# Pooling with a user's rows in eight partitions, 32-column weights in four column groups, and normalisation after the pooling

## The chip, the cores and the metric

The kernel runs on one core of a Trainium2 chip. Its time is the device time in microseconds (us). Weights, inputs and outputs lie in the chip's memory (HBM) before and after.

## The reference

Everything is float32. For 1024 users there are 50 history rows of 300 numbers each (`x`) and 200 label rows of 300 numbers (`label_embedding`).

```python
E, K, N = 300, 200, 50

def attn_pool(x, mask, w_a, b_a, w_b):            # x: [b, 50, 300]
    score = exp((x @ w_a + b_a) @ w_b)            # one number a row
    score = where(mask == 0, PAD, score)          # PAD = -2**32 + 1
    p = softmax(score, axis=1)
    return einsum('bne,bn->be', x, p)

mask = sign(sum(abs(x), axis=2))
q1 = attn_pool(x, mask, w1, b1, w2)
q2 = attn_pool(x, mask, w3, b3, w4)
h  = concat([q1, q2], 1) @ w5 + b5                # [b, 300]
f6 = h @ w6 + b6
g  = (v @ v.T)[iu, ju]                            # upper triangle, 44850 pairs
f7 = (h[:, iu] * h[:, ju] * g) @ w7 + b7
out8 = concat([f6, f7], 1) @ w8 + b8
return einsum('bu,bku->bk', out8, label_embedding)
```

## The kernel before

The users are taken in four groups of 256 (`G = 4`, `GB = 2` tiles of 128 users each). A group passes through stages, and a program written out by hand puts stages of neighbouring groups beside each other. There are six stretches, called phases here: -1 (the head), 0, 1, 2, 3, and 4 (the tail). In phases 0 to 3 a loop over 89 **units** (`NU`) runs the pair products of group `ph`: a unit is up to four tiles of 128 pairs. For a unit the vector engine (DVE) multiplies transposed rows of `h` by rows that a DMA brings back from a copy in HBM (`products`, L739: `sring` and `hT` into `cring`, four slots), the scalar engine (ACT) multiplies the unit's rows of `w7` by `g` (`w7_scale`, L600), and TensorE (PE) takes 4 tiles x 2 matmuls with 128x128 weights and 300 columns from them (`unit`, L466). Between the units stand the pooling of group `ph + 1` (none in phase 3), and on DVE the label products of group `ph - 1` (`label_row`, L766; phases 1 to 4, the tail holds nothing else). The head pools group 0, the first thing that must be done.

**Pooling** goes in **halves** of 64 users (four to a group, `GS = 4`, 16 in all). A user's 50 rows lie in two partitions, 25 rows in each (`T = N // 2`), in five chunks of 5 rows (`XT`, `XCH`), in a ring of eight chunk slots (`XSLOTS`). DVE makes two dot products of each row (`score_row`, L679, 50 steps a half, `XROWS`), ACT the sum of absolute values of each (`absolute`, L540, 25 a half). Then ACT takes the exponential (`exps`), DVE masks and takes the maximum, over two partitions by one shuffle with the neighbour (`maxima`, L703), ACT the softmax's exponential with its sum (`softexp`), DVE adds the two partitions' sums, divides, and spreads the weights into matrices [128 partitions x 128 columns], one for each of the 25 rows (`normalise`, L719, `wts`). `pool_chunk` (L435) on PE multiplies: 25 matmuls a half with 128x128 weights and 300 columns, five after each of five units. ACT copies the result (`pools_out`), PE transposes it (`turn`), ACT copies again (`pools_turned`), and after the fourth half `mix` (L444) multiplies by `w5` (18 matmuls); the result is stored to HBM (`rows_out`, on GpSimd's queue) and read back in shifted rows (`s_load`, L302).

What stands where is set by pairs of numbers, (steps after a half's last row in the head, the same in the phases), and every engine walks through the same steps:

```python
        EXP, SOFT, MAX, NORM = (0, -1), (1, 0), (1, 1), (2, 3)
        POOL = [(3, 3 + c) for c in range(XCH)]
        POOL_OUT, TURN, TURN_OUT = (4, 8), (5, 8), (6, 9)
        MIX, MIX_OUT = (7, 10), (8, 11)
        X_LOAD = [(4, 6 + c) for c in range(XCH)]
```

In a phase the x rows are spread over the first 68 units (a half ends with unit 16, 33, 50 and 67), the label rows over units 8 to 88, so that DVE has as many rows in each. In the head a step has `HEAD_ROWS = 5` rows. Loads of x and labels and of `sring` are all issued by SyncE (SP), in one queue, in this order, each after the wait that frees its slot; the loads of `w7` by ACT.

Of the kernel before, what the change touches and what calls it, by code (L numbers as in the profile page):

```python
# [87 lines left out]
def rec_kernel(nc, x, label, w13, w24, w5, w6, w8, bcols, b8, w7p, vleft, vright, out):  # L88
# [10 lines left out]
    T = N // 2  # L99
# [3 lines left out]
    XT = 5  # L103
    XCH = T // XT
    XROWS = 2 * T
    XSLOTS = 8
# [11 lines left out]
    HEAD_ROWS = 5  # L118
# [4 lines left out]
    with ctx:  # L123
# [17 lines left out]
        wts = sb("wts", [P, T, 2, P // 2])  # L141
# [6 lines left out]
        onehot = sb("onehot", [P, P // 2])  # L148
# [5 lines left out]
        small = sb("small", [P, 3, 2, 3 * T + 8])  # L154
        junk = sb("junk", [P, 2, 2, E], BF16)
        absjunk = sb("absjunk", [P, 2, E], BF16)
        absum = sb("absum", [P, 3, T])
        masked = sb("masked", [P, 3, T])
# [35 lines left out]
        prob_done = sem("prob_done")  # L194
# [15 lines left out]
        dots = [small[:, k, :, 0:T] for k in range(3)]  # L210
        expo = [small[:, k, :, T:2 * T] for k in range(3)]
        prob = [small[:, k, :, 2 * T:3 * T] for k in range(3)]
        maxi = [small[:, k, :, 3 * T:3 * T + 1] for k in range(3)]
        maxo = [small[:, k, :, 3 * T + 1:3 * T + 2] for k in range(3)]
        nmax = [small[:, k, :, 3 * T + 2:3 * T + 3] for k in range(3)]
        part = [small[:, k, :, 3 * T + 3:3 * T + 4] for k in range(3)]
        parto = [small[:, k, :, 3 * T + 4:3 * T + 5] for k in range(3)]
        total = [small[:, k, :, 3 * T + 5:3 * T + 6] for k in range(3)]
        recip = [small[:, k, :, 3 * T + 6:3 * T + 7] for k in range(3)]

        x_v = x.rearrange("(s b) (f t) e -> s (b f) t e", b=P // 2, f=2)
# [6 lines left out]
        HEAD_STEPS = GS * XROWS // HEAD_ROWS  # L228
        TAIL_STEPS = GB * LC

# [40 lines left out]
        def last_step(ph):  # L271
            return {-1: x_end(-1, GS - 1) + 14, G: TAIL_STEPS}.get(ph, NU)
# [12 lines left out]
        def _(sp):  # L285
# [5 lines left out]
            def x_load(n):  # L291
                s, c = n // XCH, n % XCH
                sp.dma_start(xring[:, n % XSLOTS], x_v[s, :, c * XT:(c + 1) * XT, :]).then_inc(x_in[n % XSLOTS], 16)
# [42 lines left out]
            for n in range(XSLOTS):  # L336
                x_load(n)
# [8 lines left out]
            for ph in range(-1, G + 1):  # L346
# [5 lines left out]
                for u in range(last_step(ph)):  # L352
# [12 lines left out]
                    for c in range(XCH):  # L365
                        for s in after_half(ph, u, *X_LOAD[c]):
                            n = ((ph + 1) * GS + s) * XCH + c
                            if n + XSLOTS < NS * XCH:
                                sp.wait_ge(x_used, n + 1)
                                x_load(n + XSLOTS)  # L370

        @block.gpsimd
        def _(pool):
# [8 lines left out]
            step(nc.gpsimd.memset(onehot[:], 0.0))  # L382
            step(nc.gpsimd.affine_select(out=ident[:], in_=ident[:], compare_op=ALU.not_equal, fill=1.0,
                                         base=0, pattern=[[-1, P]], channel_multiplier=1))
            for f in range(2):
                step(nc.gpsimd.affine_select(out=onehot[:], in_=onehot[:], compare_op=ALU.not_equal,
                                             fill=1.0, base=-f, pattern=[[-2, P // 2]], channel_multiplier=1))
# [31 lines left out]
        def _(pe):  # L419
# [242 lines left out]
        def _(dve):  # L662
# [37 lines left out]
            def carry():  # L700
                nc.vector.memset(tick[:], 0.0)
# [139 lines left out]
```

## Time and profile before

| | |
|---|---|
| median of three runs | 2047.17 us (2040.95 to 2052.43) |
| the profiled execution | 2043.87 us |
| its span on the core | 2041.7 us |
| PE busy (matmuls) | 1760.3 us, 86% |
| DVE busy | 1455.3 us, 71% |
| ACT busy | 863.3 us, 42% |
| DMA | 629.75 MB, 308 GB/s over the span |
| pooling matmuls, records on PE | 800 |
| x score rows on DVE | 800 |

A float32 matmul leaves two records on PE, each with a weight load (LDWEIGHTS, engine PEld) of its own: 400 pooling matmuls are 800 records. The engines work beside each other, so their busy times don't add up to the span; what counts is which of them the others wait for in a given phase. The head lasts from 0 to 164.3 us, the phases 0 to 3 end at about 588, 1033, 1482 and 1868 us, and the tail is the rest.

### The profile page before, as it was taken

The numbers are of one execution on the slowest core, as the hardware profiler recorded it, in microseconds if no ns is written. First come the engines' busy times: TensorE is split into PE (matmuls) and PEld (weight loads), VectorE is DVE, ScalarE is ACT, GpSimd is POOL, SyncE is SP. The second block draws the span as 40 slices with busy tenths as digits, with TensorE's granted clock in tenths as the row PEclk, the third lists the DMA queues.
The fourth block names the chain that finished last, engine by engine and source line by source line (L and its number), as shares of the span: only waits on it lengthen the run. The fifth ranks groups of instructions, "written<-read, shape, count | busy, mean of one in ns | idle before, by whom it ended". The sixth has DMA issues, their size and how long they took to land.

```text
span 2041.7 us, 23493 instructions
## 1 busy us (share of the span) xinstructions
PE 1760.3 (86%) x6820; PEld 1290.3 (63%) x6820; DVE 1455.3 (71%) x5499; ACT 863.3 (42%) x2413; POOL 22.7 (1%) x49
## 2 busy tenths in 40 slices
PE   3567999999999999999979999999889999998000
PEld 2345777777767777777657777777667777775000
DVE  8835645544147888988558898888536777773998
ACT  3525545545345564553345454553234444442000
POOL 0000000000000000000000000000000000000000
PEclk9788999999999999999989999999899999997555
DMA  6358566666566999999968999989869999995997
GB/s 223 126 165 315 190 234 238 219 242 237 193 240 241 359 354 379 354 382 405 350 246 303 361 340 392 348 340 389 273 252 356 404 406 408 409 391 178 392 395 310
DMA packets 121789, 629.75 MB, mean 308 GB/s; under 512 B 14136, under 2 KB 24921, under 8 KB 99133
## 3 DMA queue, kind: packets, MB, share of 16 engines
q1 hardware_dynamic: 93853, 408.04, 53.0%
q10 hardware_dynamic: 26208, 217.10, 28.0%
q0 software_dynamic: 1600, 3.10, 0.5%
q8 instruction: 55, 0.90, 0.2%
q14 instruction: 73, 0.60, 0.1%
HBM read 625.09 MB, written 3.10 MB: 308 GB/s over the span
## 4 chain that ended last, share of the span: by engine, by line
PE 79%; DVE 11%; DMA 6%; ACT 2%; issue 2%; POOL 0%; SPq 0%; DVEq 0%; ACTq 0%; POOLq 0%
PE bank L480 64%; PE bank L440 10%; DVE lring L775 8%; DMA sring<-hrows 3%; DMA lring<-in_label 2%; DMA wring<-in_w7p 2%; PE bank L452 1%; DVE junk L688 1%; ACT absjunk L546 1%; PE bank L462 1%; PE bank L490 1%; PE bank L488 1%; DVE cring L755 1%; ACT wring L608 1%; PE bank L432 0%
## 5 line engine op out<-in xcount | busy, mean ns | idle before, releaser
L480 PE MATMUL bank<-wring,cring 128*128 128x300 f32 x5616 | 1448.2, 419 | 38.9 <-DVE cring L755 38.2
L480 PEld LDWEIGHTS bank<-wring,cring 128*128 128x128 f32 x5616 | 1072.7, 192 | 398.7 <-DVE cring L755 40.1
L608 ACT ACTIVATE wring<-wring,gcol 128x300 f32<-128x300 f32 x1404 | 642.0, 532 | 786.6 <-PE bank L480 497.2
L755 DVE TENSOR_TENSOR cring<-hT,sring 128x1024 f32<-128x1024 f32 (+1 forms) x344 | 418.1, 1216 | 432.6 <-PE bank L480 386.6
L775 DVE SCALAR_TENSOR_TENSOR lring<-lring,out 128x300 f32<-128x300 f32 x1600 | 644.7, 465 | 29.9 <-DMA lring<-in_label 16.2
L688 DVE SCALAR_TENSOR_TENSOR junk<-xring,ubc 128x300 bf16<-128x300 f32 x800 | 328.1, 463 | 0.0
L440 PE MATMUL bank<-xring,wts 128*128 128x300 f32 x800 | 221.4, 429 | 64.9 <-DVE wts L733 64.9
L440 PEld LDWEIGHTS bank<-xring,wts 128*128 128x128 f32 x800 | 157.0, 197 | 119.2 <-issue 59.7
L546 ACT ACTIVATE absjunk<-xring 128x300 bf16<-128x300 f32 x400 | 174.9, 439 | 0.2
L775 DVE DVE_READ_ACCUMULATOR lring<-lring,out 128x1 f32 x1600 | 129.9, 81 | 0.0
L546 ACT ACTIVATION_READ_ACCUMULATOR absjunk<-xring 128x1 f32 x400 | 75.4, 189 | 0.0
L688 DVE DVE_READ_ACCUMULATOR junk<-xring,ubc 128x1 f32 x800 | 64.3, 80 | 0.0
L733 DVE TENSOR_TENSOR wts<-small,onehot 128x640 f32<-128x640 f32 x80 | 60.2, 819 | 0.6
L755 DVE TENSOR_TENSOR cring<-sring 128x1024 f32<-128x1024 f32 (+1 forms) x12 | 11.5, 956 | 62.4 <-issue 43.9
L535 ACT ACTIVATE flat<-bank 128x300 f32<-128x300 f32 x24 | 9.6, 414 | 108.8 <-PE bank L440 91.5
L452 PE MATMUL bank<-poolT,w5sb 128*128 128x256 f32 (+1 forms) x144 | 39.3, 403 | 0.7 <-issue 0.7
L707 DVE TENSOR_SCALAR masked<-absum 128x25 f32<-128x25 f32 x16 | 2.9, 178 | 42.6 <-ACT absjunk L546 33.4
L452 PEld LDWEIGHTS bank<-poolT,w5sb 128*128 128x128 f32 (+1 forms) x144 | 20.2, 164 | 19.1 <-issue 16.3
L432 PE MATMUL bank<-ident,flat 128*128 128x128 f32 (+1 forms) x72 | 12.9, 304 | 15.3 <-ACT flat L535 15.3
L432 PEld LDWEIGHTS bank<-ident,flat 128*128 128x128 f32 (+1 forms) x72 | 8.5, 140 | 21.4 <-ACT flat L535 19.1
L462 PE MATMUL bank<-hT,w6sb 128*128 128x256 f32 (+3 forms) x72 | 19.5, 399 | 0.0
L560 ACT ACTIVATE small<-small 128x25 f32<-128x25 f32 x32 | 9.8, 308 | 22.6 <-DVE small L717 22.6
(49 smaller groups left out, 182.9 us busy)
## 6 DMA issues: line engine op xcount, KB each, us to landing
lring<-in_label SPq DMA_DIRECT2D x320, 750.0 KB, 7.2
wring<-in_w7p ACTq DMA_DIRECT2D x168, 1200.0 KB, 8.0
sring<-hrows SPq DMA_DIRECT2D x172, 512.0 KB
xring<-in_x SPq DMA_DIRECT2D x80, 750.0 KB, 5.8
wring<-in_w7p ACTq DMA_DIRECT2D x8, 1050.0 KB, 8.1
sring<-hrows SPq DMA_DIRECT2D x16, 176.0 KB
sring<-hrows SPq DMA_DIRECT2D x16, 132.0 KB
sring<-hrows SPq DMA_DIRECT2D x8, 160.0 KB
```

The costliest lines, as they stand in the source:

```text
L432: mm = pe.transpose(dst[0:n, c * P:(c + 1) * P], src[:, o:o + n], ident[:])
L440: mm = pe.matmul(pooled[s % 2][:, 0:E], wts[:, t].rearrange("p h b -> p (h b)"), xring[:, (s * XCH + c) % XSLOTS, t % XT, :], start=(t == ...
L452: mm = pe.matmul(dst[0:n, 0:L], w5sb[0:nk, q, o:o + n], poolT[0:nk, q % NCH, q // NCH, :], start=(q == 0), stop=(q == 2 * NCH - 1))
L462: mm = pe.matmul(dst[0:n, 0:L], w6sb[0:nk, c, o:o + n], hT[0:nk, g % 2, c, :], start=(c == 0), stop=(c == NCH - 1))
L480: mm = pe.matmul(acc[(g * GB + b) % 4][:, 0:E], lhs, w, start=(t == 0), stop=(t == NT - 1))
L488: pe.matmul(dst[:, 0:E], f6T[0:n, c, b * P:(b + 1) * P], w8sb[0:n, c, :], start=False, stop=False)
L546: nc.scalar.activation(absjunk[:, k % 2, :], xring[:, n % XSLOTS, t % XT, :], ACT.Abs, accum_out=absum[:, s % 3, t:t + 1]).then_inc(abs_do ...
L608: ins = nc.scalar.activation(w, w, ACT.Copy, scale=gcol[:, t:t + 1])
L688: ins = nc.vector.scalar_tensor_tensor(out=junk[:, k % 2, r % 2, :], in0=xring[:, n % XSLOTS, t % XT, :], scalar=1.0, in1=ubc[:, hd, 0:E], ...
L733: nc.vector.tensor_tensor(wts[:, t0:t1], prob[k][:, :, t0:t1].rearrange("p h t -> p t h").unsqueeze(3).to_broadcast([P, XT, 2, P // 2]), o ...
L755: nc.vector.tensor_tensor(cut(cring[:, k % CSLOTS]), in0, cut(sring[:, nb % SSLOTS]), ALU.mult).then_inc(c_ready, 1)
L775: ins = nc.vector.scalar_tensor_tensor(out=row_in, in0=row_in, scalar=1.0, in1=out8[:, m % (2 * GB), :], op0=ALU.mult, op1=ALU.mult, accum ...
```

## The change

A user's 50 rows now lie in **eight** partitions (`FOLD = 8`), six in each, and the two rows left over in a seventh place of the first two of the eight; the seventh place of the other six is set to zero once, at the start. A half of 64 users becomes four **parts** of 16 users (`PARTS`, `UB`), each a chunk of seven rows (`XT = 7`) in a ring of six (`XSLOTS`). A half has 28 places a partition and not 25 (`TT`), and so 56 score rows and 28 sums of absolute values. The weights of one place are a matrix [128 x 32]; the matmul of part j writes partitions 32j to 32j + 31 of the PSUM bank, and the four parts of a place follow each other on PE.

A chunk comes with three DMAs: one of six rows for all partitions, and two of one row for 16 partitions each. At the start the six large ones are issued first and the twelve small ones behind them. The maximum now goes over eight partitions (three shuffles), and is subtracted on DVE. The weights are not normalised: DVE writes them in one instruction and sums them (`weights`), PE adds four small matmuls (2 columns) that sum over partitions, and after the pooling DVE takes the denominator and its reciprocal (`denominators`), which ACT applies when it copies the pooled rows.

```diff
-    XT = 5
-    XCH = T // XT
-    XROWS = 2 * T
-    XSLOTS = 8
+    FOLD = 8
+    UB = P // FOLD
+    M = 2 * UB
+    PARTS = P // 2 // UB
+    TM, LEFT = N // FOLD, N % FOLD
+    T = TM + 1
+    TT = PARTS * T
+    CUTS = [(0, T)] if T <= 7 else [(0, 7), (7, T)]
+    CHUNK = [(j, t0, t1) for j in range(PARTS) for t0, t1 in CUTS]
+    XT = max(t1 - t0 for _, t0, t1 in CHUNK)
+    XCH = len(CHUNK)
+    XROWS = 2 * TT
+    XSLOTS = 6
-    HEAD_ROWS = 5
+    HEAD_ROWS = 7
...
-        EXP, SOFT, MAX, NORM = (0, -1), (1, 0), (1, 1), (2, 3)
-        POOL = [(3, 3 + c) for c in range(XCH)]
-        POOL_OUT, TURN, TURN_OUT = (4, 8), (5, 8), (6, 9)
-        MIX, MIX_OUT = (7, 10), (8, 11)
-        X_LOAD = [(4, 6 + c) for c in range(XCH)]
+        EXP, SOFT, MAX, WEIGH = (0, 0), (1, 1), (1, 1), (2, 2)
+        POOL, DEN, POOL_OUT = (2, 3), (3, 4), (3, 4)
+        TURN, TURN_OUT = (4, 5), (4, 6)
+        MIX, MIX_OUT = (5, 7), (5, 8)
+        X_LOAD = (3, 4)
...
-                sp.dma_start(xring[:, n % XSLOTS], x_v[s, :, c * XT:(c + 1) * XT, :]).then_inc(x_in[n % XSLOTS], 16)
+                if main:
+                    rows = src[:, 0:FOLD * TM, :].rearrange("b (f t) e -> b f (t e)", f=FOLD)
+                    z = min(t1, TM)
+                    sp.dma_start(slot[:, 0:z - t0, :].rearrange("p t e -> p (t e)"),
+                                 rows[:, :, t0 * E:z * E]).then_inc(s, 16)
+                if left and t1 == T:
+                    for f in range(LEFT):
+                        sp.dma_start(slot[f:P:FOLD, TM - t0, :], src[:, FOLD * TM + f, :]).then_inc(s, 16)
...
             for n in range(XSLOTS):
-                x_load(n)
+                x_load(n, left=False)
+            sp.wait_ge(vconsts, 1)
+            for n in range(XSLOTS):
+                x_load(n, main=False)
...
-                    for c in range(XCH):
-                        for s in after_half(ph, u, *X_LOAD[c]):
+                    for s in after_half(ph, u, *X_LOAD):
+                        sp.wait_ge(x_used, (ph + 1) * GS + s + 1)
+                        for c in range(XCH):
                             n = ((ph + 1) * GS + s) * XCH + c
                             if n + XSLOTS < NS * XCH:
-                                sp.wait_ge(x_used, n + 1)
                                 x_load(n + XSLOTS)
...
-            def pool_chunk(s, c):
-                if c == 0 and s >= 2:
+            def pool_rows(s):
+                if s >= 2:
                     pe.wait_ge(pool_out, s - 1)
-                pe.wait_ge(wts_done, s * XCH + c + 1)
-                for t in range(c * XT, (c + 1) * XT):
-                    mm = pe.matmul(pooled[s % 2][:, 0:E], wts[:, t].rearrange("p h b -> p (h b)"),
-                                   xring[:, (s * XCH + c) % XSLOTS, t % XT, :], start=(t == 0), stop=(t == T - 1))
+                pe.wait_ge(wts_done, 2 * (s + 1))
+                dst = pooled[s % 2]
+                for t in range(T):
+                    for j in range(PARTS):
+                        c = next(c for c in range(XCH) if CHUNK[c][0] == j and CHUNK[c][1] <= t < CHUNK[c][2])
+                        pe.matmul(dst[j * M:(j + 1) * M, 0:E], wts[:, j * T + t].rearrange("p h b -> p (h b)"),
+                                  xring[:, (s * XCH + c) % XSLOTS, t - CHUNK[c][1], :], start=(t == 0), stop=(t == T - 1))
+                for j in range(PARTS):
+                    mm = pe.matmul(dst[j * M:(j + 1) * M, E:E + 2], both[:].rearrange("p h b -> p (h b)"),
+                                   part[s % 3][:, :, j], start=True, stop=True)
                 mm.then_inc(x_used, 1)
...
             def pools_out(s):
-                act.wait_ge(x_used, (s + 1) * XCH)
-                cp(flat[:, s % 2, :], pooled[s % 2][:, 0:E]).then_inc(pool_out, 1)
+                act.wait_ge(den_done, 2 * (s + 1))
+                nc.scalar.activation(flat[:, s % 2, :], pooled[s % 2][:, 0:E], ACT.Copy,
+                                     scale=den[:, s % 2, 1:2]).then_inc(pool_out, 1)
...
+            def denominators(n):
+                dve.wait_ge(x_used, n + 1)
+                nc.vector.scalar_tensor_tensor(
+                    out=denjunk[:], in0=pooled[n % 2][:, E:E + 2], scalar=1.0, in1=headmask[:], op0=ALU.mult,
+                    op1=ALU.mult, accum_out=den[:, n % 2, 0:1]).then_inc(den_done, 1)
+                dve.wait_ge(den_done, 2 * n + 1)
+                nc.vector.reciprocal(den[:, n % 2, 1:2], den[:, n % 2, 0:1]).then_inc(den_done, 1)
```

**PE, phase 0.** L440 and L469 are the pooling, L480 and L512 the units, L432 and L457 the transposes, L472 the small sums. Before, from the last chunk of the first half to the first of the second:

```order
L440 MATMUL bank<-xring,wts 128x300 x5
L480 MATMUL bank<-wring,cring 128x300 x8
L432 MATMUL bank<-ident,flat 128x128 x2
L432 MATMUL bank<-ident,flat 44x128
L480 MATMUL bank<-wring,cring 128x300 x96
L440 MATMUL bank<-xring,wts 128x300 x5
L480 MATMUL bank<-wring,cring 128x300 x8
```

Now, from before the first half's pooling to the second's:

```order
L512 MATMUL bank<-wring,cring 128x300 x72
L469 MATMUL bank<-xring,wts 32x300 x28
L472 MATMUL bank<-small,both 32x2 x4
L512 MATMUL bank<-wring,cring 128x300 x16
L457 MATMUL bank<-ident,flat 128x128 x2
L457 MATMUL bank<-ident,flat 44x128
L512 MATMUL bank<-wring,cring 128x300 x120
```

Five groups of five matmuls with a unit between them became one group of 28 and one of four.

**DVE, head, end of the first half.** L717 and L758 end the maximum, L688 and L728 are score rows, L733 and L767 write the weights. Before:

```order
L717 TENSOR_SCALAR small<-small 128x2
L688 SCALAR_TENSOR_TENSOR junk,small<-xring,ubc 128x300 x5
L701 MEMSET tick 128x1
L723 STREAM_SHUFFLE small<-small 128x2
L724 TENSOR_TENSOR small<-small 128x2
L725 RECIPROCAL small<-small 128x2
L726 TENSOR_TENSOR small<-small 128x2x25
L733 TENSOR_TENSOR wts<-small,onehot 128x640 x5
L688 SCALAR_TENSOR_TENSOR junk,small<-xring,ubc 128x300 x45
```

Now:

```order
L758 TENSOR_TENSOR small<-small 128x2x28
L728 SCALAR_TENSOR_TENSOR junk,small<-xring,ubc 128x300 x7
L767 TENSOR_TENSOR wts<-small,onehot 128x896
L770 TENSOR_REDUCE small<-small 128x2x4
L728 SCALAR_TENSOR_TENSOR junk,small<-xring,ubc 128x300 x7
L775 SCALAR_TENSOR_TENSOR denjunk,den<-bank,headmask 128x2
L779 RECIPROCAL den<-den 128x1
L728 SCALAR_TENSOR_TENSOR junk,small<-xring,ubc 128x300 x42
```

The normalisation in front of the weights is gone, and L775, seven rows behind the weights, waits for the pooling on PE.

**SP, phase 0, the x loads behind the first half.** L311 and L337 load `sring`. Before:

```order
L311 DMA sring<-hrows 128x1024 [waits c_ready] x11
L293 DMA xring<-in_x 128x1500 [waits x_used]
L311 DMA sring<-hrows 128x1024 [waits c_ready]
L293 DMA xring<-in_x 128x1500 [waits x_used] x2
L311 DMA sring<-hrows 128x1024 [waits c_ready]
L293 DMA xring<-in_x 128x1500 [waits x_used] x2
```

Now:

```order
L337 DMA sring<-hrows 128x1024 [waits c_ready] x10
L315 DMA xring<-in_x 128x1x1800 [waits x_used]
L319 DMA xring<-in_x 16x300 x2
L315 DMA xring<-in_x 128x1x1800
L319 DMA xring<-in_x 16x300 x2
```

Five loads, each behind its own chunk's matmuls, became a block of four chunks (twelve DMAs) behind one wait.

## Rows read from the trace of the kernel before

**Rows 1.** Costliest groups: line engine op, xcount | busy us, mean ns | idle before.
```profile
L480 PE MATMUL bank<-wring,cring 128*128 128x300 f32 x5616 | 1448.2, 419 | 38.9 <-DVE cring L755 38.2
L775 DVE SCALAR_TENSOR_TENSOR lring<-lring,out 128x300 f32<-128x300 f32 x1600 | 644.7, 465 | 29.9 <-DMA lring<-in_label 16.2
L440 PE MATMUL bank<-xring,wts 128*128 128x300 f32 x800 | 221.4, 429 | 64.9 <-DVE wts L733 64.9
```

**Rows 2.** Windows: length; busy PE, PEld, DVE, ACT, POOL; clock, DMA, GB/s.
```profile
0.00:164.30 164.30, 74.44 (x252) 50.19 (x252) 106.41 (x493) 62.91 (x263) 5.69 (x17) 0.83 0.53 183
164.30:588.00 423.70, 423.66 (x1669) 314.90 (x1670) 210.27 (x585) 204.86 (x573) 4.21 (x8) 0.99 0.64 230
588.00:1033.00 445.00, 433.61 (x1705) 319.22 (x1704) 356.99 (x1362) 216.24 (x606) 4.76 (x9) 0.99 0.91 345
1033.00:1482.00 449.00, 435.49 (x1703) 320.47 (x1702) 361.50 (x1376) 215.19 (x603) 5.30 (x11) 0.98 0.89 335
```

**Rows 3.** Timeline of PE, phase 1, a unit and chunks: start us, us.
```profile
944.73 4.20 PE L480 MATMUL bank<-wring,cring 128*128 128x300 f32 x16
948.77 2.69 PE L440 MATMUL bank<-xring,wts 128*128 128x300 f32 x10
951.30 4.20 PE L480 MATMUL bank<-wring,cring 128*128 128x300 f32 x16
```

**Rows 4.** Timeline of PEld in phase 0: the mix, loads of changing shape.
```profile
541.80 0.73 PEld L452 LDWEIGHTS bank<-poolT,w5sb 128*128 128x128 f32 x4 [0.33 <-issue]
542.87 0.29 PEld L452 LDWEIGHTS bank<-poolT,w5sb 44*128 44x128 f32 x2 [0.33 <-issue]
543.49 0.59 PEld L452 LDWEIGHTS bank<-poolT,w5sb 128*44 128x44 f32 x4 [0.33 <-issue]
```

**Rows 5.** Weight loads by shape, whole run: busy us, mean ns.
```profile
L440 PEld LDWEIGHTS bank<-xring,wts 128*128 128x128 f32 x800 | 157.0, 197 | 119.2 <-issue 59.7 <-DVE wts L733 12.1
L452 PEld LDWEIGHTS bank<-poolT,w5sb 128*44 128x44 f32 x32 | 3.2, 119 | 4.5 <-issue 2.9
```

**Rows 6.** Timeline of PE, head: poolings, mix, first unit.
```profile
38.00 15.46 PE L440 MATMUL bank<-xring,wts 128*128 128x300 f32 x50 [30.28 <-DVE wts L733]
66.37 14.96 PE L440 MATMUL bank<-xring,wts 128*128 128x300 f32 x50 [11.85 <-DVE wts L733]
120.86 15.00 PE L440 MATMUL bank<-xring,wts 128*128 128x300 f32 x50 [10.85 <-DVE wts L733]
137.59 9.88 PE L452 MATMUL bank<-poolT,w5sb 128*128 128x256 f32 x36 [0.67 <-issue]
164.34 5.86 PE L480 MATMUL bank<-wring,cring 128*128 128x300 f32 x12 [16.87 <-DVE cring L755]
```

**Rows 7.** Timeline of DVE, head, first half: rows, maximum, weights.
```profile
11.32 0.46 DVE L688 SCALAR_TENSOR_TENSOR junk<-xring,ubc 128x300 bf16<-128x300 f32 x1
11.71 0.46 DVE L688 SCALAR_TENSOR_TENSOR junk<-xring,ubc 128x300 bf16<-128x300 f32 x1
32.86 0.17 DVE L707 TENSOR_SCALAR masked<-absum 128x25 f32<-128x25 f32 x1
33.95 0.16 DVE L716 TENSOR_TENSOR small<-small 128x2 f32<-128x2 f32 x1
34.22 0.46 DVE L688 SCALAR_TENSOR_TENSOR junk<-xring,ubc 128x300 bf16<-128x300 f32 x1
37.03 3.77 DVE L733 TENSOR_TENSOR wts<-small,onehot 128x640 f32<-128x640 f32 x5
```

**Rows 8.** DMA, 0 to 30 us: KB, median us to landing; x ring.
```profile
DMA packets 3254, 9.42 MB, mean 314 GB/s; under 512 B 464, under 2 KB 1965, under 8 KB 3253
xring<-in_x SPq DMA_DIRECT2D x8, 750.0 KB, 11.7
wring<-in_vleft ACTq DMA_DIRECT2D x1, 702.0 KB, 4.2
DMA to landing us min/median/max: 4.1/5.8/16.4
```

**Rows 9.** Waits on DVE, 940 to 1070 us: us, times, longest.
```profile
DVE lring L775 <- DMA lring<-in_label: 11.5, 6, 3.1
```

**Rows 10.** Timeline of DVE, then PE, end of phase 1.
```profile
1005.19 1.23 DVE L755 TENSOR_TENSOR cring<-sring 128x1024 f32<-128x1024 f32 x1 [3.57 <-issue]
1024.95 1.23 DVE L755 TENSOR_TENSOR cring<-sring 128x1024 f32<-128x1024 f32 x1 [14.25 <-issue]
1026.23 7.22 PE L480 MATMUL bank<-wring,cring 128*128 128x300 f32 x20 [9.55 <-DVE cring L755]
```

More of the change, by code:

```diff
@@ L98, in rec_kernel @@
     L = GB * P
-    T = N // 2
     NS = 2 * NBT
     GS = 2 * GB
-    XT = 5
-    XCH = T // XT
-    XROWS = 2 * T
-    XSLOTS = 8
+    FOLD = 8
[11 more added lines that the diff above has]
+    XSLOTS = 6
+    ROUNDS = [1 << k for k in range(FOLD.bit_length() - 1)]
     LR = 5
@@ L208, in rec_kernel, with x_landed @@
         out_stored = [sem(f"out_stored{k}") for k in range(2)]
[L210 to L221, printed above, removed]
+        dots = [small[:, k, :, 0:TT] for k in range(3)]
+        expo = [small[:, k, :, TT:2 * TT] for k in range(3)]
+        prob = [small[:, k, :, 2 * TT:3 * TT] for k in range(3)]
+        maxi = [small[:, k, :, 3 * TT:3 * TT + PARTS] for k in range(3)]
+        maxo = [small[:, k, :, 3 * TT + PARTS:3 * TT + 2 * PARTS] for k in range(3)]
+        part = [small[:, k, :, 3 * TT + 2 * PARTS:3 * TT + 3 * PARTS] for k in range(3)]
+        by_part = lambda a: a.rearrange("p h (j t) -> p h j t", t=T)
+        x_v = x.rearrange("(s b) n e -> s b n e", b=UB)
         label_v = label.rearrange("(m p) (c r) e -> m p c r e", p=P, r=LR)
         out_v = out.rearrange("(m p) k -> m p k", p=P)
-        HEAD_STEPS = GS * XROWS // HEAD_ROWS
         TAIL_STEPS = GB * LC
+        ROWS = [(c, t, hd) for c, (_, t0, t1) in enumerate(CHUNK) for t in range(t0, t1) for hd in range(2)]
+        def x_landed(n):
+            loads = lambda m: 1 + LEFT if CHUNK[m % XCH][2] == T else 1
+            return 16 * sum(loads(m) for m in range(n % XSLOTS, n + 1, XSLOTS))
         def x_rows_by(ph, u):
@@ L505, in _ @@
                         unit(ph, u)
-                    for c in range(XCH):
-                        for s in after_half(ph, u, *POOL[c]):
-                            pool_chunk((ph + 1) * GS + s, c)
+                    for s in after_half(ph, u, *POOL):
+                        pool_rows((ph + 1) * GS + s)
                     for s in after_half(ph, u, *TURN):
@@ L674, in _ @@
             dve.wait_ge(u_ready, 2)
-            dve.wait_ge(consts, 5)
-            SWAP = [q ^ 1 for q in range(32)]
+            dve.wait_ge(consts, 2)
+            nc.vector.tensor_reduce(onehot[:], ident[:].rearrange("p (u f) -> p u f", f=FOLD), AX.X,
+                                    ALU.add).then_inc(vconsts, 1)
+            nc.vector.tensor_reduce(headmask[:], ident[:].rearrange("p (j h u) -> p h j u", h=2, u=UB), AX.XY,
+                                    ALU.add).then_inc(vconsts, 1)
+            dve.wait_ge(vconsts, 6)
+            nc.vector.tensor_copy(both[:], onehot[:].unsqueeze(1).to_broadcast([P, 2, UB])).then_inc(vconsts, 1)
+            dve.wait_ge(vconsts, 7)
             def score_row(s, r):
-                c, hd, t = r // (2 * XT), r % (2 * XT) // XT, r // (2 * XT) * XT + r % XT
+                c, t, hd = ROWS[r]
+                at = CHUNK[c][0] * T + t
                 n = s * XCH + c
-                if r % (2 * XT) == 0:
-                    dve.wait_ge(x_in[n % XSLOTS], 16 * (n // XSLOTS + 1))
-                k = s * T + r // 2
+                if t == CHUNK[c][1] and hd == 0:
+                    dve.wait_ge(x_in[n % XSLOTS], x_landed(n))
+                k = s * TT + r // 2
                 if r % 2 == 0 and k >= 2:
@@ L720, in normalise, with weights @@
+            def weights(n):
                 k = n % 3
                 dve.wait_ge(prob_raw, n + 1)
[L722 to L727 removed]
@@ L728, in normalise @@
[L728 to L737 removed]
+                if n >= 1:
+                    dve.wait_ge(x_used, n)
@@ L790, in _ @@
                         maxima((ph + 1) * GS + s)
-                    for s in after_half(ph, u, *NORM):
-                        normalise((ph + 1) * GS + s)
+                    for s in after_half(ph, u, *WEIGH):
+                        weights((ph + 1) * GS + s)
+                    for s in after_half(ph, u, *DEN):
+                        denominators((ph + 1) * GS + s)
 def kernel(**inputs):
```

104 lines of the change are left out of this document (49 added, 55 removed).

## The prediction

> **What bounds the kernel now.** I read the windows by phase first. In phases 0 to 2 PE is busy for all but 0, 11 and 14 us, at a granted clock of 0.98 to 0.99 of 2.4 GHz, so there PE sets the pace; DVE stands beside it with 210 us in phase 0 but 357 and 362 us in phases 1 and 2 (80%), where DMA moves 345 and 335 GB/s at a share of 0.9 [rows 2]. In the head PE is busy for 74 of 164 us. There the timeline has the poolings 26.5 to 28.4 us after one another, each waiting for DVE's weights [rows 6], and DVE makes score rows without a gap [rows 7]: the head is DVE's, up to the last pooling. Of PE's time the units' records hold 1448 us and the pooling's 800 records 221 [rows 1]; a gain can only come from the latter. Phase 3 and the tail have no pooling and stay as they are. So the change can gain on PE in the 12 halves of phases 0 to 2, and act on the head through DVE, the x loads and the last pooling.
>
> **PE, the pooling.** Now ten records (five matmuls) take from 948.77 to 951.30 us, 0.2525 us a record, and a unit of 16 records 4.04 us at the same pitch [rows 3]. A half costs 50 x 0.2525 = 12.6 us. The change makes 28 matmuls of it, 56 records. The trace has no two matmuls that lie on different columns of the array, so the price is bounded. From above, one after another: 56 x 0.2525 = 14.1 us, since it is the 300 columns that pass through that cost, not the width of the weights (in the mix two records more of 256 columns cost 1.07 - 0.62 = 0.45 us, whatever the shape [rows 4]). From below, all four parts at once: 14.1 / 4 = 3.5 us. I take the middle way, two at once, 7.1 us: the two records of one matmul need the same 32 columns and stand one behind the other in the queue, so if PE starts matmuls in the order of the queue, only the second record of one part and the first of the next can run together. Then come the four small matmuls, 8 records: below, nearly nothing; above, one narrow weight load of 0.119 us each [rows 5], 0.95 us; I take 0.7. And the array changes shape twice a half: in the mix four records of 128 rows and two of 44 take 1.07 + 0.62 = 1.69 us, where six at 0.225 would take 1.35, so a switch costs 0.17 us [rows 4], two of them 0.35. Together P = 8.2 us a half (bounds 4.6 and 15.4) in place of 12.6. **12 halves: -53 us** (bounds -96, +34).
>
> The Trainium skill (TensorE: Matmul & The Clock Gate, The mechanism) says that a weight load overlaps a running matmul only where the row groups differ, and all groups here have the same 128 rows. The rows speak against it: loads of 0.197 us for the same 128 rows lie under records that follow each other every 0.2525 us [rows 3, 5]. By the rule each record would have its load of about 0.119 us on top, 56 x 0.37 = 21 us a half, and the 12 halves would cost 100 us and not gain; I leave that out of the sum.
>
> **The head.** Five steps.
> (1) The rows start later. Before they start at 11.3 us [rows 7]. Now the small loads of the first chunk stand in the queue behind six large ones: 6 x 128 x 7200 bytes = 5.5 MB, and 1.4 MB of `vleft` and `vright`, 7.0 MB. The 9.42 MB of the first 30 us came in about 22 us [rows 8], some 415 GB/s, so they land at 2 + 17 = 19 us. Rows start at 19.3, +8.
> (2) A row costs 0.392 us on DVE (11.32 to 11.71 [rows 7]); 56 take 22.0 us and not 19.6.
> (3) Between the last row and the pooling stand two steps of 7 rows (2.7 us each, before 2.0), the maximum, 1.36 us now (32.86 to 34.22 [rows 7]) and 0.8 more for two shuffles and maxima (0.2 each with their gaps), and the weights: 896 columns in one instruction, about 1.0 us by 0.75 for 640 (3.77 for five [rows 7]), and a small sum, 1.3. First pooling: 19.3 + 22.0 + 2.7 + 2.2 + 2.7 + 1.3 = 50.2 us, before 38.0 [rows 6].
> (4) The halves follow each other more slowly. Six slots hold one and a half halves; the third and fourth chunk of a half are loaded only after the whole pooling of the half before. So the period is: P in the head; the third chunk with its three DMAs, 4.8 us (shortest landing 4.1 [rows 8], with 0.96 MB for 0.77 and three issues); 28 rows, 11.0; then 2.7 + 2.2 + 2.7 + 1.3 as above: 24.7 + P. In the head PE comes from a long wait and begins at its lower level (1.2 GHz): the poolings take 15.0 us there for 12.6, so I add 2.4 to P, 10.6 (the head's granted clock is 0.83 [rows 2]). Period 35.3 us, before 27.6 (three from 38.0 to 120.86 [rows 6]).
> (5) Behind the last half there are no rows between, -5.5: last pooling from 50.2 + 3 x 35.3 - 5.5 = 150.6 to 161.2 us, before to 135.9. The denominators put 0.5 us in front of the copy. From there to the first unit (28.5 us now [rows 6]) nothing changes.
> **Head: +26 us.** In general 4P - 7.
>
> **Phases 1 and 2, the loss of DVE's lead.** DVE may be four units ahead of PE (`CSLOTS`). Now `denominators` makes it wait in each half for the pooling behind the unit just before; from there it is 4.0 - 0.5 - 1.2 = 2.3 us ahead. In phase 0 it wins the lead back at once. In phases 1 and 2 a step is a product (1.15) and 7.4 rows, 4.05 us, against a unit's 4.04: it does not. What the lead covered comes to PE: maxima and weights of the next half, 3.5 us against 2.3, 1.2 x 6 = 7 us; waits for label loads, 11.5 us at the end of phase 1 [rows 9]; and at a phase's end the products of unit 86 at 1005.2 us, from which the last `sring` loads take 20 us, a wait of 9.6 us on PE already [rows 10], which 5 us less lead makes 5 longer, twice. The block of four x chunks (3.8 MB, some 10 us of DMA at these rates) stands in SP's queue ahead of labels and `sring`, which have 20 us to come; covered, if barely. Bounds 5 and 45; **+20 us**, near the lower one because the pooling itself is still 8 us in which DVE can work.
>
> Nothing: DVE's weights (five instructions less one, 2.7 us a half, against 6 more rows, 2.4 us), ACT's three more sums of absolute values, 2 us a half on an engine with half its time free in every phase [rows 2].
>
> **Sum:** -53 + 26 + 20 = -7 us against the profiled execution's 2043.9, 2037. That execution lies 3.3 us under the median of the runs, so I give **2040 us**. With P open the sum is 16P - 158 + the loss of lead (20): the change gains if a half's pooling takes less than 8.6 us. My forecast sits on that point, and half a per cent, 10 us, is what a measurement of this kernel can tell from no change.
>
> **Rivals.**
> *All four parts run together.* P = 4.6. For it: the parts touch neither each other's columns nor partitions. Against: the two records of a matmul share their columns and stand together in the queue. -96 us on PE, the head 4 x 4.6 - 7 = +11; but DVE with 17 steps of 4.05 and 4 us of maxima and weights, 73 us a half, now stands level with PE (17 x 4.04 + 4.6), so the lost lead costs 35: 1995 us, as a median 1998. The Trainium skill gives 2.38 times for three column tiles (TensorE: Matmul & The Clock Gate, Measured speedup vs the span model), which for four would be nearer to this case than to mine; no row here shows it.
> *The parts run one after another*, the case that ends slower. P = 15.4: +34 on PE, head +55, lost lead 5 to 10 (DVE has more time): 2140 us. For it: no row shows two matmuls at once, and all four write the same PSUM bank. It decides from P over 9.2 us on.
> *The pairs overlap only in part*, P about 11: +16 x 11 - 158 + 15 = 2077, as a median 2080.
> *The side effects are not as I take them:* the small x loads don't wait behind the large ones (-8), the lead is kept (-15): 2014 to 2017, inside my own range.
>
> **Chances.** Two at once 0.50, four at once 0.14, one after another 0.22, in part 0.14. The forecast's own range is 2015 to 2075. The whole range, 1985 to 2125, leaves out most of the serial case, a little of the fastest one, and the tails. Faster by over half a per cent: 0.22 of the forecast's half (where the lead or the first loads cost less) and 0.13, 0.35. Within: 0.20. Slower: 0.10 of the forecast's, 0.21 of the serial, 0.14 in part, 0.45.
>
> **What would show it.** The time from the first pooling record of a half in phase 0 to the next unit's first: 8.2 us, 4.6 or 15.4. In the head: first score row at 19.3 us, first pooling at 50, period 35, last pooling's end at 161, first unit at 190. In phases 1 and 2: PE waits for DVE's products after the poolings, DVE for PE at the denominators, phase 0 shorter by 18 us and phases 1 and 2 by 8 each. Wrong would be the argument on the queue's order if P is under 6 or over 10, and the one on slots if the head's period is under 30 us.

## The result and the profile after

The changed kernel takes **2098.4 us** (median of four runs, 2088.8 to 2103.6) beside 2045.6 us for the kernel before on the same chip: a ratio of **1.024, 95% interval 1.021 to 1.027**. It is slower. I had forecast 2040 us, a hair faster, in a range up to 2125. One of the ten runs of e2 below took 4978 us; its ratio is made without it.

The busy times by phase, in the columns of [rows 2]:

```profile
0.00:195.75 195.75, 37.22 (x309) 18.07 (x309) 109.31 (x545) 68.24 (x281) 5.06 (x14) 0.76 0.61 152
195.75:603.00 407.25, 393.17 (x1726) 286.04 (x1726) 208.95 (x635) 207.87 (x587) 4.21 (x8) 0.98 0.73 239
603.00:1070.00 467.00, 407.65 (x1742) 290.34 (x1740) 347.94 (x1378) 219.03 (x620) 4.76 (x9) 0.95 0.93 326
1070.00:1520.00 450.00, 408.03 (x1760) 291.86 (x1760) 359.28 (x1421) 219.23 (x619) 5.30 (x10) 0.96 0.92 335
```

PE is no longer busy throughout the phases: 14, 59 and 42 us of them are idle, where there were 0, 11 and 14. The head grew from 164.3 to 195.75 us. For exact lengths I take one mark in each phase, the transposes of `flat7` in unit 1: from the first unit to the first mark phase 0 takes 419.0 us (before 433.3), from mark to mark phase 1 takes 477.0 (449.4) and phase 2 takes 451.7 (448.7), phase 3 369.7 (373.4). With the head's 31.4 that is -14, +28, +3, -4 and +31, in all +44 of the 45 us by which the span of the profiled execution grew (between the medians lie 53 us).

The pooling on PE reaches the lower bound that the prediction had for its records, 3.5 us. Timeline of PE in phase 0, to be read against [rows 3], and below it the first 0.05 us of the same half by themselves:

```profile
282.11 3.74 PE L469 MATMUL bank<-xring,wts 128*32 128x300 f32 x56
285.66 0.22 PE L472 MATMUL bank<-small,both 128*32 128x2 f32 x8
285.81 8.35 PE L512 MATMUL bank<-wring,cring 128*128 128x300 f32 x32
```
```profile
281.76 0.42 PE L512 MATMUL bank<-wring,cring 128*128 128x300 f32 x1
282.11 0.46 PE L469 MATMUL bank<-xring,wts 128*32 128x300 f32 x4
```

From 282.11 to 285.81 us are **3.7 us a half**, the small matmuls included, where it was 12.6. All four parts run at once: four records start within 20 ns of each other, the next four 0.25 us later, and so on (56 records in 3.55 us, 0.063 us each on average, a quarter of 0.2525). Over 12 halves PE is given 107 us. They are lost again, and more. Who waits for whom on PE and DVE, whole run (us, times, longest):

```profile
DVE cring L797 <- DMA sring<-hrows: 139.8, 14, 30.8
...
PE bank L512 <- DVE cring L797: 127.6, 30, 20.0
...
DVE lring L817 <- DMA lring<-in_label: 75.0, 19, 26.6
...
DVE junk L728 <- DMA xring<-in_x: 30.5, 4, 17.5
```

PE waited 38 us for products before and now 128; behind the products stand the loads of `sring`, labels and x. The head shows what is wrong with them. The DMA of the first 34 us, in 40 slices (busy share, then GB/s), of the kernel before and then of the changed one:

```profile
DMA  0088999999999999999999999999996000000000
GB/s 0 8 140 350 416 423 416 406 409 445 416 417 409 438 431 409 416 438 409 409 424 409 424 412 363 371 342 298 308 319 178 24 0 0 0 0 0 10 0 0
```
```profile
DMA  0178999998999999998999999999999999799999
GB/s 0 6 107 366 416 397 409 291 202 215 263 229 271 195 271 246 237 246 212 263 229 271 195 263 220 220 246 237 254 212 254 246 271 215 157 221 223 201 250 376
...
xring<-in_x SPq DMA_DIRECT2D x6, 900.0 KB, 18.0
xring<-in_x SPq DMA_DIRECT2D x12, 18.8 KB, 22.5
```

`vleft` and `vright` come at 410 GB/s in both. Then the x loads come at 410 GB/s before and at **about 235 GB/s** now, and the DMA engines are as busy with it (share 0.9). By the trace's packet records each packet takes longer: one of 7200 bytes 0.51 us here (median from 8 to 18 us), and 0.27 us in e1 and e6 below. The first score row is at 31.4 us, where I had said 19.3:

```profile
31.40 0.47 DVE L728 SCALAR_TENSOR_TENSOR junk<-xring,ubc 128x300 bf16<-128x300 f32 x1 [17.46 <-DMA xring<-in_x]
```

So the question of the experiments: does the halved rate of the x loads make the whole loss, and what halves it? The rivals are my own terms, the lead of DVE and the block of x loads in SyncE's queue.

### The profile page after: what moved, and what is told of

The parts are those of the page before. It is cut to its first block, busy times and chain, and to the rows that moved or that the text cites. A ratio compares the mean times of both kernels' runs of the same rounds, so it can differ in the third digit from the quotient of the medians.

```text
span 2087.0 us, 24279 instructions
## 1 busy us (share of the span) xinstructions
PE 1645.0 (79%) x7044; PEld 1175.4 (56%) x7044; DVE 1453.0 (70%) x5695; ACT 878.5 (42%) x2477; POOL 22.0 (1%) x46
## 3 DMA queue, kind: packets, MB, share of 16 engines
q10 hardware_dynamic: 26208, 217.10, 28.2%
## 4 chain that ended last, share of the span: by engine, by line
PE 47%; DVE 26%; DMA 20%; SPq 3%; issue 3%; ACT 1%; POOL 0%; DVEq 0%; ACTq 0%; POOLq 0%
PE bank L512 39%; DVE lring L817 13%; DMA sring<-hrows 8%; DMA lring<-in_label 8%; DVE junk L728 6%; DVE cring L797 5%; PE bank L469 3%; DMA xring<-in_x 2%; SPq L319 2%; DMA wring<-in_w7p 2%; PE bank L484 1%; PE bank L494 1%; SPq L315 1%; PE bank L522 1%; PE bank L520 1%
## 5 line engine op out<-in xcount | busy, mean ns | idle before, releaser
L512 PE MATMUL bank<-wring,cring 128*128 128x300 f32 x5616 | 1466.6, 423 | 130.2 <-DVE cring L797 127.6
L512 PEld LDWEIGHTS bank<-wring,cring 128*128 128x128 f32 x5616 | 1079.7, 193 | 505.8 <-DVE cring L797 141.9
L728 DVE SCALAR_TENSOR_TENSOR junk<-xring,ubc 128x300 bf16<-128x300 f32 x896 | 365.9, 463 | 30.5 <-DMA xring<-in_x 30.5
L580 ACT ACTIVATE absjunk<-xring 128x300 bf16<-128x300 f32 x448 | 195.9, 438 | 17.9 <-DMA xring<-in_x 17.6
L469 PE MATMUL bank<-xring,wts 128*32 128x300 f32 x896 | 67.6, 458 | 127.8 <-DVE small L770 127.8
L469 PEld LDWEIGHTS bank<-xring,wts 128*32 128x32 f32 x896 | 30.4, 120 | 162.7 <-issue 117.1
L580 ACT ACTIVATION_READ_ACCUMULATOR absjunk<-xring 128x1 f32 x448 | 84.1, 188 | 0.0
L728 DVE DVE_READ_ACCUMULATOR junk<-xring,ubc 128x1 f32 x896 | 71.6, 80 | 0.0
L775 DVE SCALAR_TENSOR_TENSOR denjunk<-bank,headmask 128x2 f32<-128x2 f32 x16 | 2.5, 159 | 80.9 <-PE bank L472 80.9
L597 ACT ACTIVATE flat<-bank,den 128x300 f32<-128x300 f32 x16 | 8.2, 512 | 62.4 <-DVE den L779 62.4
L457 PE MATMUL bank<-ident,flat 128*128 128x128 f32 (+1 forms) x72 | 13.2, 308 | 20.3 <-ACT flat L567 16.1
L457 PEld LDWEIGHTS bank<-ident,flat 128*128 128x128 f32 (+1 forms) x72 | 8.6, 141 | 24.8 <-ACT flat L567 17.9
L520 PE MATMUL bank<-w8sb,f6T 128*128 128x300 f32 (+1 forms) x48 | 19.2, 527 | 0.0
```

What stands on the lines that cost most here:

```text
L457: mm = pe.transpose(dst[0:n, c * P:(c + 1) * P], src[:, o:o + n], ident[:])
L469: pe.matmul(dst[j * M:(j + 1) * M, 0:E], wts[:, j * T + t].rearrange("p h b -> p (h b)"), xring[:, (s * XCH + c) % XSLOTS, t - CHUNK[c][1] ...
L512: mm = pe.matmul(acc[(g * GB + b) % 4][:, 0:E], lhs, w, start=(t == 0), stop=(t == NT - 1))
L520: pe.matmul(dst[:, 0:E], f6T[0:n, c, b * P:(b + 1) * P], w8sb[0:n, c, :], start=False, stop=False)
L580: nc.scalar.activation(absjunk[:, k % 2, :], xring[:, n % XSLOTS, t - CHUNK[c][1], :], ACT.Abs, accum_out=absum[:, s % 3, at:at + 1]).then ...
L728: ins = nc.vector.scalar_tensor_tensor(out=junk[:, k % 2, r % 2, :], in0=xring[:, n % XSLOTS, t - CHUNK[c][1], :], scalar=1.0, in1=ubc[:, ...
```

## The experiments

Times are medians beside the kernel before on the same chip (2044.7, 2045.6 and 2046.4 us in the three groups).

**e1, the load as one flat list.** The large load's source, 16 users x 8 pieces, becomes 128 pieces at one pitch. This variant reads other rows of x than the reference asks for, the same number of bytes in the same pieces.

```diff
-                    rows = src[:, 0:FOLD * TM, :].rearrange("b (f t) e -> b f (t e)", f=FOLD)
+                    rows = bass.AP(x.tensor, part0, [[TM * E, P], [1, TM * E]])
```

> The changed kernel, but each large x load reads 128 equal pieces of 7200 bytes one behind another (one pitch for all partitions) in place of 16 users by 8 pieces; it reads other rows than the reference's, and the small loads stay. Theory A (the x loads run at some 230 GB/s and not 415 because of how the load is described, users by pieces, and not for their size): the head's first score row comes at about 22 us and not at 32, the x loads go at about 400 GB/s, the head ends 15 to 20 us earlier, the whole is 20 to 45 us faster than the changed kernel. Theory B (7200-byte pieces, or reading from a close region, are slow in themselves): nothing changes, within 10 us of the changed kernel.

Measured: **1984.3 us**, ratio 0.972 (0.968 to 0.975), 114 us below the changed kernel and 3% below the one before. The head's DMA, same slices:

```profile
GB/s 0 6 189 344 416 420 407 436 420 432 407 415 441 466 407 415 424 415 407 415 424 443 277 178 291 171 337 378 311 284 205 37 10 0 0 0 0 10 0 0
```

Some 420 GB/s as long as the large x loads run (to 18 us), with pieces of 7200 bytes, from a region as close together. So it is neither the size of the pieces nor the closeness of what is read. Theory A stands so far; its gain was 114 us and not 20 to 45.

**e2, the kernel before with a load in two levels.** 64 users x 2 pieces of 6000 bytes; it reads rows 24 to 48 in place of 25 to 49.

```diff
-                sp.dma_start(xring[:, n % XSLOTS], x_v[s, :, c * XT:(c + 1) * XT, :])
+                rows = bass.AP(x.tensor, s * (P // 2) * N * E + c * XT * E, [[N * E, P // 2], [(T - 1) * E, 2], [1, XT * E]])
+                sp.dma_start(xring[:, n % XSLOTS].rearrange("p t e -> p (t e)"), rows)
```

> The kernel before, with its x loads described as 64 users by two pieces (the second piece begins one row early, so that the two levels can't be merged; it is the same number of bytes in pieces of the same 6000 bytes, but rows 24 to 48 in place of 25 to 49). Theory A: the first x loads fall from 415 to about 230 GB/s, and the kernel gets 10 to 40 us slower by that alone. Theory B: the time is that of the kernel before, within 5 us.

Measured: 2045.3 us, ratio 1.000 (0.998 to 1.002), and no lower rate in the head:

```profile
GB/s 0 6 162 311 416 416 424 410 437 409 431 409 431 424 409 431 409 438 409 409 417 416 438 405 360 340 354 290 299 330 192 38 6 0 0 0 0 0 10 0
```

Theory A as I had put it falls: two levels alone cost nothing. What is left of it is the number at the outermost level, 64 here and 16 in the change.

**e5, the kernel before with 16 x 8.** As e2 with 16 groups x 8 pieces of 6000 bytes, the groups a row closer than in the reference, so it too reads other rows.

```diff
+                rows = bass.AP(x.tensor, s * (P // 2) * N * E + c * XT * E, [[4 * N * E - E, 16], [T * E, 8], [1, XT * E]])
```

> The kernel before, with each x load described as 16 groups by 8 pieces of 6000 bytes (the groups begin one row early so that the levels can't be merged; same bytes, other rows). Theory A16 (the slow rate belongs to an outermost level of 16, so that each DMA engine gets eight neighbouring partitions; an outermost level of 64, as in the run before, does not have it): the x loads fall to about 230 GB/s in the head, the first score rows are on time or up to 2 us late, and the kernel is 10 to 60 us slower than before. Theory size (it is the 7200-byte pieces, or 57.6 KB of neighbouring reads for an engine): the time is that of the kernel before, within 5 us, and the head's rate 410 GB/s.

Measured: **2095.4 us**, ratio 1.023 (1.018 to 1.027). The kernel before, with its old pooling, its old normalisation and its old order, loses 50 us by this one description. Its DMA in the head, and PE's waits:

```profile
GB/s 0 6 107 379 416 416 418 284 210 254 219 240 226 233 219 240 226 240 226 254 226 240 226 240 233 240 226 233 219 233 229 226 233 240 254 226 261 193 217 270
```
```profile
PE bank L482 <- DVE cring L757: 70.6, 12, 17.5
```

The same 235 GB/s (230 here), with pieces of 6000 bytes that lie 30 KB apart; theory size falls. The first score row is only 1.2 us late (12.5 us), since the first chunk is alone in front. By the marks the head and phase 0 lose 3 and 2 us, phase 1 loses 45 and phase 2 loses 8. PE waits 71 us for products in place of 38.

**e6, the change with halves of users.** Each user is cut into two halves of 25 rows first, and each half into four partitions of 6 rows and one left over. The load's outermost level is then 32, and the rows left over are one load of 32 partitions. All rows are there: the softmax and the pooling do not care in which partition of its user a row lies.

```diff
-                    rows = src[:, 0:FOLD * TM, :].rearrange("b (f t) e -> b f (t e)", f=FOLD)
+                    rows = bass.AP(x.tensor, part0, [[N // 2 * E, 2 * UB], [TM * E, FOLD // 2], [1, TM * E]])
...
-                    for f in range(LEFT):
-                        sp.dma_start(slot[f:P:FOLD, TM - t0, :], src[:, FOLD * TM + f, :]).then_inc(s, 16)
+                    sp.dma_start(slot[0:P:FOLD // 2, TM - t0, :],
+                                 bass.AP(x.tensor, last, [[N // 2 * E, 2 * UB], [1, E]])).then_inc(s, 16)
```

> The changed kernel with a user's rows split first into two halves of 25 and each half into four partitions of six and one row left over. A large load is then 32 half users by 4 pieces of 7200 bytes, and the two small loads of a chunk become one of 32 partitions. All rows are the reference's. Theory A16: the x loads run at some 400 GB/s as in the flat load, SyncE issues 8 x loads a half and not 12, and the time is 1975 to 1990 us, 3% below the kernel before. Theory size: 2070 to 2100 us, as the changed kernel.

Measured: **1986.9 us**, ratio 0.970 (0.967 to 0.973). The rate in the head is 410 to 440 GB/s while the large x loads run; phase 0 takes 399.1 us by the marks, phase 1 436.3, phase 2 427.1, the head 174.5:

```profile
51.41 5.93 PE L469 MATMUL bank<-xring,wts 128*32 128x300 f32 x56 [43.33 <-DVE small L770]
82.75 5.62 PE L469 MATMUL bank<-xring,wts 128*32 128x300 f32 x56 [23.77 <-DVE small L770]
113.79 5.47 PE L469 MATMUL bank<-xring,wts 128*32 128x300 f32 x56 [23.76 <-DVE small L770]
140.01 6.00 PE L469 MATMUL bank<-xring,wts 128*32 128x300 f32 x56 [19.11 <-DVE small L770]
174.48 30.90 PE L512 MATMUL bank<-wring,cring 128*128 128x300 f32 x113 [16.22 <-DVE cring L797]
```

Against the changed kernel the head is 21 us shorter and the phases 20, 41 and 25. e1, with two small loads a chunk, and e6, with one, end within 3 us of each other, so the second small load has no price that shows here.

**e3, the parts one after another.** The pooling's two loops swapped, so that neighbours in PE's queue use the same 32 columns.

> The changed kernel with the two loops of the pooling swapped: all seven places of a part one after another, so that neighbours in the queue use the same 32 columns. If overlap needs different columns in neighbours, a half's 56 records take 14.1 us in the phases in place of 3.6, or somewhat less at the seams. If the four-fold rate were owed to the narrow weights alone, 3.6 us stay. The whole then is about 12 x 10 = 120 us slower at most.

Measured: 2204.0 us, ratio 1.078 (1.073 to 1.084). Timeline of PE, the same half:

```profile
315.75 10.63 PE L469 MATMUL bank<-xring,wts 128*32 128x300 f32 x53
325.97 0.24 PE L472 MATMUL bank<-small,both 128*32 128x2 f32 x6
326.22 0.92 PE L469 MATMUL bank<-xring,wts 128*32 128x300 f32 x3
327.10 8.35 PE L512 MATMUL bank<-wring,cring 128*128 128x300 f32 x32
```

11.35 us a half in place of 3.7, so the four-fold rate is owed to neighbours on different columns, not to narrow weights. And six records of the small matmuls, which stand behind in the queue, run at 325.97 us while three of the pooling still follow at 326.22: matmuls on different columns pass each other. That is also why it is 11.35 and not 14.1: in the trace's records, at each of the three seams, the first four records of the next part start beside the last four of the part before, which saves 12 x 0.2525 = 3.0 us.

**e4, the denominators later.** In the changed kernel, in the phases:

```diff
-        POOL, DEN, POOL_OUT = (2, 3), (3, 4), (3, 4)
-        TURN, TURN_OUT = (4, 5), (4, 6)
-        MIX, MIX_OUT = (5, 7), (5, 8)
+        POOL, DEN, POOL_OUT = (2, 3), (3, 7), (3, 7)
+        TURN, TURN_OUT = (4, 8), (4, 9)
+        MIX, MIX_OUT = (5, 10), (5, 11)
```

> The changed kernel with the denominators, the copy, the transposes and the mix three steps later in the phases (the head as it is). Theory lead (DVE's wait for the pooling takes its lead, and PE then waits for products): PE's wait for DVE falls from 128 us by 40 or more, the whole is 20 to 40 us faster. Theory queue (the block of twelve x loads holds up the loads of sring and labels behind it in SyncE's queue): PE's wait stays within 20 us of 128, and the whole within 12 us of the changed kernel.

Measured: 2099.0 us, ratio 1.026 (1.023 to 1.030), the changed kernel's time; PE waits 134 us for products. The lead was not it. That is what theory queue had said too, but this run doesn't test the block itself: it leaves the twelve loads where they are.

**e7 and e8, on top of e6.** e7 issues each small load behind its own large one at the start. e8 also takes e4's edit and spreads the four chunks' loads over four steps:

```diff
-        X_LOAD = (3, 4)
+        X_LOAD = [(3, 7 + c) for c in range(XCH)]
```

> As the halves kernel, and at the start each chunk's small load stands right behind its large one, not behind all six. Expected: the first score row at 11 to 13 us in place of 21, the first pooling at about 43, and the whole 8 us faster than the halves kernel. Rival: DVE then waits for later chunks instead, and under 3 us are gained.

> As the kernel with halves and small loads first, with the denominators, copy, transposes and mix three steps later in the phases, and the four chunks' x loads issued in four steps (7 to 10 after the half) in place of one block. With the loads at full rate the lost lead and the block are what is left: if they cost what the prediction said, 10 to 20 us faster than without; if the rate of the x loads was all of it, within 5 us, or slower since the last chunks now come later than DVE needs them.

Measured: e7 **1978.2 us**, ratio 0.966 (0.963 to 0.969), its first score row at 12.3 us and its first pooling at 43.3 us against 51.4: 8.1 us in the trace, 8.8 in the medians, as expected. e8: 1978.3 us, 0.967 (0.963 to 0.970). DVE's waits at the denominators fall from 81.5 us in e7 to 20.8, yet PE's wait for products stays (65.6 and 64.5): the lead has no price here either. The block was moved in the same run, and DVE waited 25.6 us for x in place of 6.3; so a small gain from spreading it may be hidden, and alone it was not tried.

**e9 to e11, the slots.** e9 is e7 with seven chunk slots (`w1T` lies in `wring` for its short life, which frees the room). e10 is e9, and e11 is e7, with `HEAD_ROWS = 4`.

> As the kernel with halves and small loads first, with seven chunk slots in place of six (w1 lies for its short life in the ring of w7). The prediction's step on the slots: the head's period, 31.1 us now, is set by the third chunk of a half, which is loaded only after the pooling of the half before. With seven slots only the fourth chunk waits, and DVE has 14 rows more (5.5 us) to hide it: period about 28 us, the head 8 us shorter, the whole 1970 us. Rival: DVE's own work (56 rows, 22 us, and its wait at the denominators, 7 us) holds the period at 29.5 or more, and 4 us or less are gained.

> As the seven slots, with 4 rows a step in the head and not 7. The rows that stand between a half's last row and its weights, and between the weights and the denominators, fall from 7 to 4 each: the pooling starts 2.4 us earlier in each half, and if the wait for the fourth chunk binds, the period shortens by as much, 7 us over the head; DVE waits longer at the denominators, so if DVE's own work binds, nothing is gained or 3 us are lost.

> Six slots, 4 rows a step in the head. Here the load behind the pooling binds by the prediction's step 4, so the period falls by 2 x 3 rows, 2.4 us, three times, 5 to 7 us in all: 1971 us. If DVE's own work binds, 1978 us stay.

Measured: e9 **1959.4 us, ratio 0.958 (0.956 to 0.961)**, e10 1964.1 (0.960, 0.956 to 0.963), e11 1978.1 (0.968, 0.964 to 0.971). The poolings of e9's head:

```profile
43.36 5.13 PE L467 MATMUL bank<-xring,wts 128*32 128x300 f32 x56 [35.34 <-DVE small L768]
71.58 6.36 PE L467 MATMUL bank<-xring,wts 128*32 128x300 f32 x56 [21.45 <-DVE small L768]
101.14 5.25 PE L467 MATMUL bank<-xring,wts 128*32 128x300 f32 x56 [21.54 <-DVE small L768]
125.18 5.18 PE L467 MATMUL bank<-xring,wts 128*32 128x300 f32 x56 [17.15 <-DVE small L768]
158.77 45.41 PE L510 MATMUL bank<-wring,cring 128*128 128x300 f32 x172 [16.17 <-DVE cring L795]
```

The periods fall from e7's 31.5, 31.0 and 26.4 us to 28.2, 29.6 and 24.0, and the first unit comes at 158.8 us, where e7 has 167.3 and e6 174.5: the 8 us that were expected. Behind the head, by the marks, phase 1 takes 433.9 us (e7 437.9), phase 2 424.0 (425.3) and phase 3 368.7 (373.2). Phase 3 pools nothing and no run changes it, but over the thirteen traces it takes 365.3 to 374.4 us, so differences of this size can't be laid to the slot.

In the heads the traces show which wait the edits touch. DVE waits for x 6.3 us in e7, and not at all in e9, e10 and e11; at the denominators it waits 16.1, 14.7, 20.0 and 19.3 us (e7, e9, e10, e11). The first units come at 167.3, 158.8, 164.4 and 164.2 us: e11's shorter steps take the wait for x away and lengthen the other one by 3.2, which leaves 3 us in the head and nothing in the medians (1978.1 against 1978.2), and in e10 there is no wait for x left to win, only the longer one. e10 is 5 us slower than e9 in the medians, inside both intervals.

e9 is the fastest version: 87 us (4.2%) below the kernel before, 139 below the change.

## Why the prediction was wrong

*The pooling on PE (forecast 8.2 us a half, 53 us gained).* Measured 3.7, 107 us given to PE. The step that failed is the premise that PE starts matmuls in the order of its queue, so that only two could overlap. Four records start together at 282.11 us, and e3 shows it again: records on other columns overtake. The rival with all four at once had 4.6 us and the right mechanism; I gave it 0.14. Its time, 1998 us, is near that of e6, 1987, where the x loads have their rate back. Here the Trainium skill's figure for column tiles (TensorE: Matmul & The Clock Gate, Measured speedup vs the span model) pointed the right way, and the measured factor for four is 4.0. The Trainium skill's rule that a weight load overlaps a running matmul only where the row groups differ (TensorE: Matmul & The Clock Gate, The mechanism), which I had left out of the sum, does not hold here: the 56 loads of a half, 0.11 us each (6.2 us in all), lie within the 3.55 us of its 56 records.

*What carries the result, the rate of the x loads, is not in the prediction.* With PE's 107 us and the head's 31 as measured, the sum needs 123 us lost in phases 0 to 2, where I had 20. The prediction took 415 GB/s for the x loads, from rows of the kernel before, whose load is described otherwise: 128 pieces at one pitch. The diff shows the new description, and I counted its bytes and not its shape. With a 16 at the outermost level the rate is 235 GB/s, so the 14.7 MB of large loads in the head and in each of three phases take 63 us of all 16 DMA engines and not 36. Where DMA had spare time (phase 0, share 0.64) it costs waits for `sring` behind the block, 20 us by e6; where it had none (phases 1 and 2, share 0.9) 41 and 25. e1 gives back 114 us by nothing but the description, e6 111 with one small load less a chunk, and e5 shows that the description alone costs the kernel before 50 us. So the cause is shown from both sides. Its price is not the same on both: 111 us in the changed kernel, 50 in the one before, and that e5 ends at 1.023, close to the change's 1.024, is chance.

*The head (+26 forecast, +31.4 measured).* Step 1 failed for the reason above: rows from 31.4 us, not 19.3. With the rate restored (e6) rows start at 20.4 us and the first pooling at 51.4, forecast 19.3 and 50.2; the queue order is right and worth 8 us (e7). Steps 3 and 4: with P at 3.7 the forecast's period is 24.7 + 3.7 + 2.4 = 30.8 us. The changed kernel has 32.6, 33.7 and, the last, 29.7 (DVE waits 13 us for x in the three), e6 has 31.3, 31.0 and 26.2, and its whole head is 10 us longer than before, where 4P - 7 gives 8. The slots bind, but by less than step 4 had it: the wait for x is 6.3 us over the three periods of e7, and right behind it stands DVE's own work with its wait at the denominators (e9 to e11). So step 4's chain through the third chunk's load came near the measured period, but it is not what alone sets it.

*The loss of DVE's lead (20 us) was not found.* e4 and e8 move the wait for the denominators away and gain nothing, at the slow rate and at the full one. The step that failed is that this wait takes from DVE what PE then lacks. Yet phases 1 and 2 give back only 13 and 22 us of their 36 in e6, together 37 us short of PE's gain, where phase 0 gives 34 of 36. The rival with four at once had put 35 us there, for a DVE level with PE. In phase 1 of e6 PE still waits 28 us for DVE, and DVE 26 us for labels and 22 for PE; whether DVE's own pace or the DMA is the last bound there was not tried.

*The range* held the time, as it took in serial columns. That is luck: the mechanism that made it 2098 was in none of its cases.

## What to carry to other kernels

Count a moved DMA by its description as well as by its bytes: put the levels of source and destination beside each other before and after, and where the outermost count falls to 16 for 128 partitions, split it otherwise (here halves of users, 32 x 4) or measure it alone. Small matmuls on different 32-column groups run four at once if neighbours in the queue lie on different groups; the order of the loops is worth a factor of three here (3.7 against 11.35 us). When the engine that sets the pace is relieved, look at what feeds it: of the 107 us freed on PE 69 showed in the phases, and only after the loads behind DVE ran at full rate.

## What was not expected of the hardware

**A load to 128 partitions with 16 entries at the source's outermost level runs at 235 GB/s, with 32 (e6), 64 (e2) or 128 (e1) at 410.** The slow rate was seen with pieces of 6000 (e5) and of 7200 bytes. In every run the levels make 128 in all, so whether the 16 outside or the 8 within is what counts can't be told apart here. The Trainium skill (DMA: Bandwidth & Descriptors, The descriptor swizzle) says that in a full 128-partition transfer each DMA engine writes four neighbouring partitions and the four that lie 32 further, all at one port of the on-chip memory. If with 16 entries each engine takes one entry, it writes eight neighbouring partitions, so two ports, and shares each with another engine; if all go through their partitions in step, half of the ports stand idle at any time, and half the rate would follow. No run here shows which engine writes what, so this stays an inference.

**A load in two levels also costs SyncE time:** 0.33 us an issue for the flat load (median of the 80 before), 0.54 us for the 80 of e2, 0.59 us for the large and the small ones of the change; twelve hold the queue from 286.0 to 294.2 us. What stands in front counts too: e1's flat loads take 0.33 us as the first of a block and 0.58 us right behind a small one. It had no measurable price: e2 stays at the time of before.

**Records on different column groups pass each other** (e3), where one might take PE for a strict queue; and a switch of the array's shape, priced at 0.17 us from the mix, costs less. The pooling's first record starts 0.345 us after the unit's last, by the trace's records, and so 0.09 us later than the pitch of 0.2525; pooling, small matmuls and both switches together are 3.8 us, of which 3.55 are the pooling.
